# Self-attention of a two-layer cross-attention model: both accumulators leave PSUM in one copy, and GpSimd scales them in two halves

## The reference, cut to what matters

```python
q = (xq @ Wq).reshape(B, N, HEADS, D_HEAD)          # xq = xc = _ln(x, g1, b1)
k = (xc @ Wk).reshape(B, S, HEADS, D_HEAD)
v = (xc @ Wv).reshape(B, S, HEADS, D_HEAD)
scores = jnp.einsum('bnhd,bshd->bhns', q, k) * D_HEAD ** (-0.5)
attn = jax.nn.softmax(scores, axis=-1)
out = jnp.einsum('bhns,bshd->bnhd', attn, v).reshape(B, N, HEADS * D_HEAD)
x = out @ Wo + bo + x
```

## Time and profile before

| | before |
|---|---|
| median of 3 runs | 2293.42 us (2293.42 to 2293.97) |
| profiled execution | 2292.69 us, its span 2290.9 us |
| mean granted TensorE clock | 0.98 |
| TensorE busy | 2121.8 us (93%) |
| VectorE busy | 1608.8 us (70%) |
| ScalarE busy | 1482.3 us (65%) |
| GpSimd busy | 1070.5 us (47%) |

### The profile page before, as it was taken

One profiled execution on the slowest core, in us unless ns is written; L12 is line 12 of the kernel. 1 busy time (PEld: TensorE's weight loads), 2 busy tenths in 40 slices (PEclk: granted clock), 3 DMA queues, 4 the chain that ended last, 5 costly groups with the idle time before them and its releaser, 6 DMA issues. The chain is left out here.

```text
span 2290.9 us, 31305 instructions
## 1 busy us (share of the span) xinstructions
PE 2121.8 (93%) x11628; PEld 1771.6 (77%) x11628; DVE 1608.8 (70%) x2345; ACT 1482.3 (65%) x2154; POOL 1070.5 (47%) x819
## 2 busy tenths in 40 slices
PE   6868999988899999999999999999997799999998
PEld 4657888876687778777777777777776689888987
DVE  5576767753787787777877778778776766666553
ACT  5546888754777777777777777777774355554431
POOL 2154544441354454454544545545454665656432
PEclk8989999998999999999999999999999999999999
DMA  6810000010000100001001000010004411111000
GB/s 212 297 43 5 22 22 22 20 66 33 19 24 16 37 15 24 24 15 34 15 15 34 15 29 24 15 33 15 24 26 165 138 44 53 56 56 47 10 10 19
DMA packets 84280, 102.67 MB, mean 45 GB/s; under 512 B 29664, under 2 KB 61152, under 8 KB 83616
## 3 DMA queue, kind: packets, MB, share of 16 engines
q1 hardware_dynamic: 84128, 100.66, 13.3%
HBM read 65.50 MB, written 33.82 MB: 43 GB/s over the span
## 5 line engine op out<-in xcount | busy, mean ns | idle before, releaser
L146 PE MATMUL PS<-R 128*128 128x512 f32 (+1 forms) x2944 | 1026.4, 349 | 77.1 <-DVE R L162 46.1
L148 PE MATMUL PS<-R 128*128 128x512 f32 (+1 forms) x2944 | 996.5, 338 | 0.0
L147 PE MATMUL PS<-R 128*128 128x512 f32 (+1 forms) x2944 | 995.8, 338 | 0.0
L146 PEld LDWEIGHTS PS<-R 128*128 128x128 f32 x2944 | 565.8, 192 | 189.9 <-DVE R L162 55.3
L156 ACT ACTIVATE R<-PS 64x512 fp32r<-64x512 f32 (+4 forms) x860 | 460.1, 548 | 239.7 <-PE PS L1805 129.4
L148 PEld LDWEIGHTS PS<-R 128*128 128x128 f32 x2944 | 565.1, 192 | 60.4
L147 PEld LDWEIGHTS PS<-R 128*128 128x128 f32 x2944 | 566.9, 193 | 54.4
L162 DVE TENSOR_TENSOR R<-F,R 128x1024 fp32r<-128x1024 f32 (+2 forms) x416 | 465.2, 1123 | 44.2 <-ACT R L156 22.4
L159 POOL TENSOR_SCALAR R<-F 128x1024 fp32r<-128x1024 f32 (+1 forms) x295 | 266.2, 904 | 284.0 <-DVE F L1958 149.3
L1500 ACT ACTIVATE F<-PS 128x1024 f32<-128x1024 f32 x256 | 263.1, 1028 | 170.3 <-DVE R L162 115.1
L159 POOL TENSOR_SCALAR R<-R 64x512 fp32r<-64x512 f32 x128 | 142.8, 1129 | 391.4 <-ACT R L156 391.4
(11 more groups left out here) (89 smaller groups left out, 1990.9 us busy)
## 6 DMA issues: line engine op xcount, KB each, us to landing
F<-sd SPq DMA_DIRECT2D x128, 128.0 KB, 2.8
xs<-F SPq DMA_DIRECT2D x16, 512.0 KB, 2.6
F<-xs SPq DMA_DIRECT2D x16, 512.0 KB, 3.6
gd<-F SPq DMA_DIRECT2D x8, 768.0 KB, 3.6
vd<-F SPq DMA_DIRECT2D x8, 768.0 KB, 5.9
R<-gd SPq DMA_DIRECT2D x6, 1024.0 KB, 5.5
R<-vd SPq DMA_DIRECT2D x6, 1024.0 KB, 5.7
F<-in_x SPq DMA_DIRECT2D x8, 512.0 KB, 5.7
```

The source lines that it names most:

```text
L146: nc.tensor.matmul(o, L[0], Rr[0], start=start, stop=False, skip_group_check=share)
L147: nc.tensor.matmul(o, L[0], Rr[1], start=False, stop=False, skip_group_check=share)
L148: return nc.tensor.matmul(o, L[1], Rr[0], start=False, stop=stop, skip_group_check=share)
```

## The change

ScalarE copies banks 4 and 5 whole, in one instruction of 128x1024, to `OAB`, which is `OA` and `OB` side by side. `OA` then holds the first head's output above and its sums below, `OB` the second head's sums above and its output below. GpSimd multiplies the upper half of `OA` in place, and the lower half of `OB` into the lower half of `OA`, as two instructions of 64x512; the second has waits for GpSimd's own earlier instructions, and it alone signals `o_mul`. The event `d_sum` is gone: SyncE's DMAs of the sums wait for the whole copy, and the first of them reads from `OA` instead of `OB`. The copy has the one wait for `o3_lo` ahead of everything.

```diff
--- before.py
+++ after.py
@@ -411,6 +411,7 @@
             o3_s = [ra.pair(NT) for _ in range(2)]
             wk = fa.take(6 * 512)
             pst3 = [wk[:, 1024 * i:1024 * i + 1024] for i in range(2)]
+            OAB = wk[:, 2048:3072]
             OA, OB = wk[:, 2048:2560], wk[:, 2560:3072]
             RS3 = fa.take(NT)
             M3 = fa.take(4, 128)
@@ -1198,7 +1199,7 @@
         c3_mm, e3 = event("c_mm", 4 * N3), event("exp", 4 * N3)
 
         p3_act, p3_pool, p3_lo = event("p_act", 2 * N3), event("p_pool", 2 * N3), event("p_lo", 4 * N3)
-        d3_mm, d3_sum, d3_out = event("d_mm", 4 * N3), event("d_sum", N3), event("d_out", N3)
+        d3_mm, d3_out = event("d_mm", 4 * N3), event("d_out", N3)
         rec3, mul3, o3_hi, o3_lo = event("rec", N3), event("o_mul", N3), event("o_hi", N3), event("o_lo", N3)
         o3_mm, o3_add = event("o_mm", N3), event("x_add", N3)
         sum3 = [event(f"sum_in{i}", N3, 16) for i in range(2)]
@@ -1307,9 +1308,9 @@
                             nc.sync.dma_start(RS3[64 * h:64 * h + 64, :], sd[k][512 * h:512 * h + 512]
                                               .partition_broadcast(64)).then_inc(in3[k].sem, 16)
                     if ok(d, N3) and j == 3:
-                        sp.wait_ge(d3_sum, d)
+                        sp.wait_ge(d3_out, d)
                         sp.wait_ge(rec3, d - 2)
-                        nc.sync.dma_start(SQ3[d % 2][0:64, :], OB[64:65, :]).then_inc(sum3[d % 2].sem, 16)
+                        nc.sync.dma_start(SQ3[d % 2][0:64, :], OA[64:65, :]).then_inc(sum3[d % 2].sem, 16)
                         nc.sync.dma_start(SQ3[d % 2][64:128, :], OB[0:1, :]).then_inc(sum3[d % 2].sem, 16)
                     e = s - 3
                     if j == 1 and ok(e, N3) and e % 8 == 7:
@@ -1536,11 +1537,8 @@
                         act.wait_ge(d3_mm, 4 * d + 3)
                         act.wait_ge(sum3[(d - 1) % 2], 2 * ((d - 1) // 2) + 1)
                         wait_weights(act, "o1")
-                        act_copy(OB[64:65, :], bank(4)[64:65, :])
-                        act_copy(OB[0:1, :], bank(5)[0:1, :]).then_inc(d3_sum.sem, 1)
                         act.wait_ge(o3_lo, d - 1)
-                        act_copy(OA[0:64, :], bank(4)[0:64, :])
-                        act_copy(OA[64:128, :], bank(5)[64:128, :]).then_inc(d3_out.sem, 1)
+                        act_copy(OAB, bank(4, 2)).then_inc(d3_out.sem, 1)
                     if ok(u, N3) and j == 3:
                         act.wait_ge(nm3_mm, u)
                         act.wait_ge(c3_mm, 4 * (u - 2) + 3)
@@ -1694,7 +1692,14 @@
                         f = d - 1
                         pool.wait_ge(in3[f % 2], 2 * (f // 2) + 1)
                         pool.wait_ge(d3_out, f)
-                        nc.gpsimd.tensor_tensor(OA, OA, RS3, ALU.mult).then_inc(mul3.sem, 1)
+                        nc.gpsimd.tensor_tensor(OA[top, :], OA[top, :], RS3[top, :], ALU.mult)
+                        pool.wait_ge(o3_lo, f - 1)
+                        pool.wait_ge(p3_pool, 2 * t if more else 2 * N3 - 1)
+                        if more and p == 5:
+                            pool.wait_ge(ln_rstd, 18 + b)
+                        if f == N3 - 1:
+                            pool.wait_ge(ln_nl, norm4[2][2])
+                        nc.gpsimd.tensor_tensor(OA[low, :], OB[low, :], RS3[low, :], ALU.mult).then_inc(mul3.sem, 1)
                         pool.wait_ge(mul3, f)
                         pool.wait_ge(o3_mm, 2 * ((f - 2) // 2) + 1)
                         pool_copy(o3_s[f % 2][0], OA).then_inc(o3_hi.sem, 1)
```

## The result

The changed kernel takes 2318.11 us (median of 4 runs, 2315.82 to 2319.93), the kernel before 2293.42: ratio 1.0111, 95% interval 1.0093 to 1.0128. It is slower by about 25 us, where 2296 was forecast and the first rival (halves in turn) gave 2315. Its profiled execution took 2319.10 us, 26.4 more than before's 2292.69.

A forecast was written before the change was run, and what follows sets the result against it. TensorE, busy 772 of 800 us, bounds the self-attention, with VectorE and GpSimd in the step's circle of waits. +2.7 (B) +2.0 (A) -2.0 (norm) +0.3 (last round) = +3.0 us, forecast 2296; own range 2290 to 2301, overall 2289 to 2318.

The forecast's parts named there:

- first rival: GpSimd's two multiplication halves run one after the other: B +1.27, A -0.71 us a turn, +21.8 us, 2315 us; chance 0.28.
- part 3: GpSimd's split multiplication: halves overlap, the second adds 0.15 us; +2.7 us in B, +2.0 in A turns.
- B turn: Short self-attention step, some 30 of 64, 17.8 us, ending with output matmuls that need GpSimd's o3_lo; forecast 0.09 us longer.
- A turn: Long self-attention step, 22 of 64, 18.57 us on average; forecast 0.09 us longer.
- Part 1: ScalarE: one wide copy at 1.03 us replaces four at 2.27, freeing 1.24 us a step; 1.3 and 2.0 us won.
- VectorE's limit: In A turns, the end of VectorE's rest L162 plus 8.98 us; 18.51 us with ScalarE's limit gone.
- norm turns: 7 A steps with a layer norm, 20.3 us each; ScalarE's shorter copy was to win 0.28 us each, 2.0 in all.
- Part 2: The sums' path: their DMAs leave after the whole copy; slack over 3 us, so no cost.
- The sign of being wrong: For part 2: the reciprocal L1615 shows idle time before it for a DMA.
- The B law: A B turn lasts until the end of GpSimd's rest L165 plus 8.42 us.
- The step from 1108.83: Step of the kernel before whose multiplication came 1.5 us late; L162 took 1.94 us, the step 19.23.
- ScalarE's limit: In A turns, ScalarE's four copies run into negation and q copies without idle time; 18.53 us a turn.

The follow-up runs named there:

- wide copy alone: The changed kernel with one multiplication of OA, the product's lower half made of the sums, second head's output left out; 2289.80 us, ratio 0.9987 to the kernel before.
- halves alone: The kernel before with its four ScalarE copies, only the multiplication split into two halves of OA; 2334.46 us, ratio 1.0184.
- the run with the waits ahead: The changed kernel with GpSimd's four own waits moved ahead of the first half, nothing between the multiplications; 2317.09 us, ratio 1.0106 to the kernel before.

## Why the prediction was wrong

**The step that failed** is in part 3, "What the second half adds is therefore between 0 and 1.29 us": 0.15 was taken, near the lower end, and 1.34 was right (1.28 and a gap of 0.06), 0.05 above the upper end. The argument was that the halves share no partition and that nothing makes the second wait; in fact the second started when the first was over. So a B turn, forecast at 0.09 us more, took 1.18 more by median, and an A turn, also forecast at 0.09 more, took 0.70 less. The Trainium skill, "GPSIMD Engine Reference", "Instruction dispatch", lets each core begin the next instruction when its own share is finished. That four cores would do the upper half while the other four do the lower was worked out from that sentence; the section doesn't state it. For two multiplications on different partitions no gain of that kind shows here, with waits between them or without: the copy behind them starts 2.72 us after the first in both kernels. What in GpSimd keeps the second half back is open. The rows nearest to the case, the pairs of 64x512 copies in turn, would have given the right end; I set them aside because a pair shared its partitions, and put a reading that no row bore out in their place. Whether other operations, or more instructions in a row, overlap on different partitions was not tried.

**What held.** With the halves in turn the first rival's terms are nearly the measured ones:

| term | forecast | first rival | measured |
|---|---|---|---|
| B, per turn | 17.9 | 19.09 | 19.00 |
| A, per turn | 18.65 | 17.85 | 17.85 |
| norm, change per turn | -0.28 | -0.28 | -0.29 |
| total | +3.0 | +21.8 | +24.7 (medians), +26.4 (profiled) |

Its shortfall on the profiled execution is 4.6 us: 2.4 in the B turns, 1.3 in the A turns, 1.0 outside them. 30 x 1.27 was 38.1; the sum of B turns rose by 40.5 although the usual one rose by 1.18 only: the two turns of 21.32 and 21.81 make 5.1 us of it above 19.00 each. In A three late turns (18.90, 18.20, 17.97) make 1.5 us. The rival took every turn as a usual one, and it did not say that a first half later than about 5.7 us into a B turn may lose the port to L162 between the halves (an estimate: L162 is due 7.05 us in, and the second half 1.34 us after the first).

**Part 1** (ScalarE frees 1.24 us a turn, of which VectorE's limit leaves 0.06 in A, 0.28 in norm turns, nothing in B; -3.3 us): right. The wide copy alone gave a ratio of 0.9987, 3 us, with A at 18.51 and norm turns 0.27 shorter.

**Part 2** (the later sums cost nothing): right for the 59 turns. VectorE had no idle time before any of the 60 reciprocals L1613 from 620 to 1750 us. The sign of being wrong that the prediction gave did show at the very end: the last three reciprocals waited 0.79, 3.79 and 5.14 us for the sums' DMA, where before the last two waited 0.98 and 4.52. With the wide copy alone the last three wait too (0.81, 4.39, 2.36), and the stretch behind the 59 turns is 573.4 us against 573.2 before, so no cost of it shows.

**The B law** (a turn is the end of L165 plus 8.42): right. At 1006.18 L165 ends 10.56 us in, which gives 18.98; the turn took 18.96. Of the 30 B turns 27 keep to it within 0.03 us; the exceptions are the first of all, 0.08 short, and the two late ones.

**The trace's own warning.** The step from 1108.83 was, but for its cause, a turn of the changed kernel: GpSimd's product 1.5 us late, L162 at 1.94 us, the turn at 19.23. It gave the first rival its right price before the run; the prediction gave that rival 0.28.

## What to carry to other kernels

When instructions are merged on one engine, price the instruction that has to be split on another, and price it whole: here 64 partitions cost GpSimd what 128 do (1.28 and 1.29 us), and two halves cost twice, also when they share no partition. Where two limits of a turn lie 0.02 us apart, as in the A turns, relieving either shows next to nothing and relieving both shows 0.7 us: look for a turn in which one of them happens to be lifted, and read the other from it. And if an instruction that nobody waits for blocks one that is on the critical path, as L165 blocked L162 in A turns, one wait can put it behind: it gave 0.66 us a turn, once ScalarE's limit was out of the way.

## What the runs showed of the hardware that was not expected

GpSimd takes two multiplications on different halves of the partitions one after the other, 1.34 us from start to start, also with no wait between them.

In the late turn from 854.04 TensorE's clock fell. After the wait of 2.08 us that ended at 865.66, this is the stretch from 866 to 870 us beside the one before it (busy time of TensorE, its weight loads, VectorE, ScalarE, GpSimd; then the granted clock, the share of DMA, GB/s):

```profile
854.00:866.00 12.00, 9.89 (x50) 7.74 (x49) 10.26 (x13) 6.72 (x10) 9.23 (x8) 1.00 0.08 24
866.00:870.00 4.00, 4.00 (x21) 3.62 (x20) 1.82 (x2) 1.83 (x3) 0.53 (x1) 0.64 0.02 1
```

A mean of 0.64 is time at 1.2 GHz among time at 2.4. L165 ended 11.47 us into that turn, so the B law gives 19.89, and the turn took 21.32: some 1.4 us stand beside the slow clock. The other late turn, from 1643.63, shows the same behind its wait of 2.79 us: a granted clock of 0.62 from 1655.9 to 1660 us, and 1.2 us more than the B law gives. So does the turn of 21.02 us of the halves alone, behind a wait of 1.80 us (0.66 from 1137 to 1142 us, 1.4 us above the law). In the usual B turn, with a wait of 1.16 us, the stretch from 1006 to 1025 us stays at 1.00. The longest wait for L165 without such a fall is the 1.73 us before 1467.49 in the run with the waits ahead, where the stretch from 1467.5 to 1472 us is at 1.00 and the turn keeps to the law within 0.02 us. Over all the profiles, the 35 B turns with a wait of 1.3 to 1.73 us for L165 keep to the law within 0.03 us, and the three with 1.80, 2.08 and 2.79 us are 1.2 to 1.4 us longer, with a slow clock behind the wait. In the two turns of the changed kernel that is 2.7 of the 26.4 us lost. That the wait caused the fall was not tested.
